# Two tiles in place of three for w2's split parts, and a sixth tile for h, in a fast-matrix-multiply feed-forward kernel

## The chip, the cores and the metric

The kernel runs on one core of a Trainium2 chip. The metric is the device time of one execution in microseconds (us); lower is better.

## The reference

The reference picks one 64x64 matrix for each of 32 samples, mixes the channels of x with it, and puts the result through a two-layer feed-forward network with a residual. All tensors are float32. Cut to what matters:

```
c   = einsum('bct,bcd->bdt', x, cond_weights[itok])   # x is 32 x 64 x 1024
h   = gelu(c @ inter_w + inter_b)                      # 1024 -> 4096
out = x + h @ output_w + output_b                      # 4096 -> 1024
```

## The kernel before

Everything but the moments at the start is matrix multiplication on TensorE (PE). Each float32 operand is split into a high part (the value rounded to the float32r type) and a low part (the value less its high part), and a product takes three matmuls: high by high, high by low, low by high. Both GEMMs are organised as fast matrix multiplications with fewer products than the plain blocking has.

**The first GEMM** makes h. Its steps are (n, c), with n from 0 to 15 (pass and group of 512 hidden columns) and c from 0 to 13. Sums and differences of blocks of h are written to two DRAM scratch tensors, `p_mem` and `q_mem`, as they are made (`keep_second` for the second pass, on the SP queue).

**The second GEMM** has 26 products t (`RANK`), each of 8 steps q (`KS`), so 208 steps. The texts number them g = 8t + q, from 0 to 207. One step multiplies a 128x512 operand of h by a 128x512 operand of w2: 4 blocks of rows (`tb`) by 3 matmuls, so 12 matmuls of 512 columns. The work of a step is spread so:

- SP (`load_h`, lines 438 to 443) loads h in pairs of steps: pair n serves steps 2n and 2n+1 and lies in one of `HRING` = 5 tiles `h_raw`. From pair 5 on, the load of pair n waits until the low parts of pair n-5 are made, since its tile is that pair's. For some products POOL adds a second block into the tile by an accumulating DMA (`add_second`, line 663).
- ACT (`high2`, lines 933 to 944) waits until step g-3 is done on PE (the ring `lhs` has `RING` = 3 tiles) and until pair g//2 is in, and writes the high part of h into `lhs` (line 939) and then that of w2 into `rhs` (line 944). `rhs` is a ring of 3 tiles as well.
- DVE (`low2`, lines 1164 to 1170) writes the low part of each (lines 1167 and 1170) when its high part is there. Behind `low2` of step g stands in DVE's order what `beside` gives it for index g-2: an update of an output tile from PSUM (`add2`, lines 1173 to 1188), or a sum of blocks of w2 for a later product (`mix`, line 1194), or nothing. For product 0 it is the trail of the first GEMM (`trail_second`, lines 1121 to 1150): up to three sums of h blocks behind a step.
- PE (`second`, lines 746 to 760) waits for both low parts of the step and runs the 12 matmuls. The PSUM banks of products t and t-2 are the same, so at the first step of product t, PE waits ahead of row block 0 for half of the updates of product t-2, and ahead of row block 2 for the rest of them. Product 16 updates four output blocks and so has 8 such instructions on DVE, indices 0 to 7 of `beside(17, i)`; the last, i = 7, stands behind `low2` of step 145, which is product 18's step 1.
- The last two steps, 206 and 207, are one piece of code, `last_two` (lines 762 to 779): the row blocks are the outer loop and the two steps the inner one, so that each output row block ends early. It waits for the low parts of both steps before its first matmul:

```
pe.wait_ge(lhs_lo, s + 2)
pe.wait_ge(rhs_lo, r + 2)
```

All waits are written out by hand. ACT and DVE work through their instructions in the order of the program, so an instruction that waits holds up all behind it on its engine. The SP queue does the same with its loads and stores; around step 0 to 12 it carries `keep_second` of group 15, the load of w2's block "30", blocks of x into the output tiles, and the pairs of h.

Of the kernel before, what the change touches and what calls it, by code (L numbers as in the profile page):

```python
# [6 lines left out]
F32R = mybir.dt.float32r  # L7
# [53 lines left out]
def build(nc, x, itok, cond_w, w1, b1, w2, b2, out):  # L61
# [12 lines left out]
    S1STEPS = GROUPS * CHUNKS  # L74
    KS = NG
    RING = 3
    WARM = 11
    HRING = 5
    PAIRS = RANK * KS // 2
    TB = 4  # L80
    NPART = 10
# [13 lines left out]
    with ExitStack() as ctx:  # L95
# [20 lines left out]
        g11, g12, g22, g21 = (at(n, 184 + 4 * i, [2, BANK]) for i, n in enumerate(("g11", "g12", "g22", "g21")))  # L116
        x1 = [at(f"x1_{j}", k, [D]) for j, k in enumerate((112, 116, 120, 124, 156, 216, 200, 184))]
        lhs = [at(f"lhs{i}", 160 + 4 * i, [2, BANK], F32R) for i in range(RING)]
        rhs = [at(f"rhs{i}", 172 + 4 * i, [2, BANK], F32R) for i in range(RING)]
        s4_w, s1_w, s2_w = (at(n, 172 + 4 * i, [KH, 2 * P]) for i, n in enumerate(("s4_w", "s1_w", "s2_w")))  # L120
        x0 = at("x0", 172, [TILES, D])
        y1_stage = [at(f"y1_stage{i}", 188 + 4 * i, [KB, P]) for i in range(2)]
        h_raw = [at(f"h_raw{i}", k, [2, BANK]) for i, k in enumerate((112, 116, 120, 124, 216))]
        part = [at(f"part{i}", 200 + 2 * i, [BANK]) for i in range(NPART)]
        part_second = {8: at("part8_second", 156, [BANK]), 9: at("part9_second", 158, [BANK])}
        y1_in = at("y1_in", 184, [4, BANK])
# [96 lines left out]
        def step2(t, q=0):  # L223
            return S1STEPS + t * KS + q
# [119 lines left out]
        def _(sp):  # L344
# [130 lines left out]
            for n in range(GROUPS):  # L475
                for c in range(CHUNKS):
                    if c == 0 and 0 < n < GROUPS - 1:
                        if n < NG - 1:
                            load_w1(n + 1)
                        elif n == NG - 1:  # L480
                            load_w1(NG + 1)
                        elif n > NG:
                            load_w1(n + 1)
                    if 0 < n <= NG:
                        keep_first(n - 1, c)
                    elif n > NG:
                        keep_second(n - 1, c)
                    if (n, c) == (1, 2):
                        for i in range(2):
                            sp.wait_ge(y1_staged[i], 32 * TB)  # L490
                        sp.dma_start(y1_in[:], y_raw_mem[0]).then_inc(y1_back, 16)
                    if y1_item(n, c) is not None:
                        keep_y1(y1_item(n, c))
                    if n == NG - 1 and c in range(4, CHUNKS, 2):
                        load_y(c // 2 - 2)
                    if n == NG and c in (0, 2):
                        load_y(5 + c // 2)
                    if n == GROUPS - 1:
                        if c == 2:
                            sp.wait_ge(lhs_lo, step1(n - 1, CHUNKS))  # L500
                            wait_kept(sp, 0, NG)
                            sp.wait_ge(c11_kept, 32 * NG)
                            wait_kept(sp, 8, NG)
                            wait_kept(sp, 9, NG)
                            for i in range(HRING):
                                load_h(i)
                        if c in (4, 6, 8):
                            sp.wait_ge(step_done, step1(n, c - 2))
                            load_w2(c // 2 - 2, ("20", "11", "10")[c // 2 - 2])
                        if c == 12:  # L510
                            sp.wait_ge(step_done, step1(n, c - 2))
                            load_x("10")

            for n in range(HRING, PAIRS):
                if n == 5:
                    for c in range(4):
                        keep_second(GROUPS - 1, c)
                    sp.wait_ge(step_done, step1(GROUPS - 1, 8))
                    load_w2(3, "30")
                if n == 6:  # L520
                    keep_second(GROUPS - 1, 4)
                    keep_second(GROUPS - 1, 5)
                if n == 7:
                    load_x("01")
                if n == 8:
                    wait_kept(sp, 8, GROUPS)
                    wait_kept(sp, 9, GROUPS)
                    for k in (1, 2, 3, 4, 5, 6, 7):
                        wait_kept(sp, k, NG)
                    for done in (c12_kept, c21_kept, c22_kept):  # L530
                        sp.wait_ge(done, 16 * NG)
                if n == 9:
                    sp.wait_ge(step_done, step1(GROUPS - 1, 12))
                    load_x("30")
                if n == 11:
                    load_x("00")
                if n == 13:
                    sp.wait_ge(rhs_lo, rhs_n(1, KS))
                    sp.wait_ge(mixed, 4)
                    load_w2(1, "31")  # L540
                if n == 16:
                    sp.wait_ge(c11_gelu, 2 * GROUPS)
                    sp.wait_ge(c12_gelu, 2 * GROUPS)
                    sp.wait_ge(c22_gelu, 2 * GROUPS)
                    load_x("31")
                if n == 18:
                    sp.wait_ge(step_done, step1(GROUPS - 1, CHUNKS))
                    load_w2(4, "01")
                if n == 20:
                    for k in range(NPART):  # L550
                        wait_kept(sp, k, GROUPS)
                    sp.wait_ge(g11_kept, 16 * NG)
                    sp.wait_ge(g22_kept, 16 * NG)
                if n == 21:
                    sp.wait_ge(lhs_lo, step1(GROUPS - 1, CHUNKS))
                    load_w2(5, "21")
                if n == 26:
                    load_x("21")
                if n == 29:
                    sp.wait_ge(rhs_lo, rhs_n(4, KS))  # L560
                    sp.wait_ge(mixed, 4 * (MIX[6] + 1))
                    load_w2(3, "00")
                if n == 34:
                    sp.wait_ge(mixed, 4 * (MIX[7] + 1))
                    load_w2(4, "20")
                if n == 37:
                    load_x("20")
                if n == 52:
                    load_x("11")
                if n == 60:  # L570
                    sp.wait_ge(acc_added, adds(12))
                    store("31")
                if n == 73:
                    sp.wait_ge(rhs_lo, rhs_n(16, KS))
                    sp.wait_ge(mixed, 4 * (MIX[18] + 1))
                    load_w2(3, "11")
                if n == 77:
                    sp.wait_ge(rhs_lo, rhs_n(17, KS))
                    load_w2(0, "10")
                if n == 80:  # L580
                    sp.wait_ge(acc_added, adds(17))
                    store("01")
                if n == 86:
                    sp.wait_ge(mixed, 4 * (MIX[20] + 1))
                    load_w2(4, "30")
                if n == 91:
                    sp.wait_ge(acc_added, adds(20))
                    store("20")
                if n == 96:
                    sp.wait_ge(acc_added, adds(21))  # L590
                    store("00")
                    store("30")
                load_h(n)
# [84 lines left out]
        def _(pe):  # L678
# [65 lines left out]
                last.then_inc(step_done, 1)  # L744

            def second(t, q):
                s, r = step2(t, q), rhs_n(t, q) % RING
                pe.wait_ge(lhs_lo, s + 1)
                pe.wait_ge(rhs_lo, rhs_n(t, q) + 1)
                for tb in range(TB):  # L750
# [11 lines left out]
            def last_two():  # L762
# [6 lines left out]
                for tb in range(TB):  # L769
                    if tb == TB - 1:  # L770
                        pe.wait_ge(acc_added, ADDED + 1)
                    for e, cols in enumerate(ENDS if tb == TB - 1 else (slice(0, BANK),)):
                        bank = bank2(t - e, tb)
                        for i in range(2):
                            for u, (a, w) in enumerate(((0, 0), (0, 1), (1, 0))):
                                last = nc.tensor.matmul(ps[:, bank, cols], lhs[(s + i) % RING][:, a, blk(tb)],  # L776
                                                        by_pairs(rhs[(r + i) % RING][:, w, :])[:, cols.start // 2:cols.stop // 2, :],
                                                        start=(e == 1 and i == 0 and u == 0),
                                                        stop=(i == 1 and u == 2), skip_group_check=True)
                        last.then_inc(tile_done, 1)  # L780
# [21 lines left out]
        def _(act):  # L802
# [128 lines left out]
                    gelu(n, 1, p, blocks(n)[2][:, p, :], c22[:, p, :], c22_gelu)  # L931

            def high2(t, q):
                s, r, n = step2(t, q), rhs_n(t, q) % RING, rhs_n(t, q) // 2
                act.wait_ge(step_done, s - RING + 1)
                act.wait_ge(h_in[n % HRING], 16 * (n // HRING + 1))
                if summed(n):
                    act.wait_ge(h_sum[n % HRING], 16 * sums(n))
                nc.scalar.activation(lhs[s % RING][:, 0, :], h_part(t, q), ACT.Copy).then_inc(lhs_hi, 1)  # L939
                if t in MIX:  # L940
                    act.wait_ge(mixed, 4 * MIX[t] + q // 2 + 1)
                elif q == 0:
# [61 lines left out]
        def _(dve):  # L1004
# [157 lines left out]
                    add_c11(n, 0)  # L1162

            def low2(t, q):
                s, r = step2(t, q), rhs_n(t, q) % RING
                dve.wait_ge(lhs_hi, s + 1)
                nc.vector.tensor_tensor(lhs[s % RING][:, 1, :], h_part(t, q), lhs[s % RING][:, 0, :].bitcast(F32),  # L1167
                                        ALU.subtract).then_inc(lhs_lo, 1)
# [194 lines left out]
```

## Time and profile before

| what | us |
|---|---|
| median of 3 runs | 1158.89 (1158.59 to 1158.95) |
| the profiled execution, its own time | 1159.22 |
| its span in the profile | 1157.4 |
| PE busy | 1152.4 |
| DVE busy | 870.2 |
| ACT busy | 561.8 |

The span is the stretch of the profile from its first to its last instruction. Busy times of the engines overlap. PE's weight loads (PEld) run beside its matmuls and are listed on their own. DMA is a mean share of 16 engines; the GB/s beside it are what they moved.

### The profile page before, as it was taken

Reading aid. Unit: us, or ns where it says so; the run is one execution under the profiler, and the core shown is the slowest. Engines: PE = TensorE matmul, PEld = TensorE weight load, DVE = VectorE, ACT = ScalarE, POOL = GpSimd, SP = SyncE. Lnnn points to the kernel's source line nnn. Section 1 sums busy time; section 2 is a strip of 40 time slices with the busy share of each in tenths; the row PEclk is TensorE's granted clock in tenths of the full one; section 3 lists DMA queues with packets and bytes.
Section 4 is the critical chain, followed back from the end, with each engine's and each line's share of the span. In section 5 each row is a group of like instructions: output and inputs, shape, how many; then the busy total and the mean of one; then the engine's idle time right before and its main releaser. Section 6 shows DMA issues by size and latency. Waiting matters only on the chain.

```text
span 1157.4 us, 15233 instructions
## 1 busy us (share of the span) xinstructions
PE 1152.4 (100%) x5468; PEld 1012.7 (87%) x5468; DVE 870.2 (75%) x1190; ACT 561.8 (49%) x963; POOL 94.7 (8%) x124
## 2 busy tenths in 40 slices
PE   9999999999999999999999999999999999999999
PEld 8988888888888888888888888888888888888887
DVE  5888787877466666666658689688899687788996
ACT  5855555555444444444445444444444444444443
POOL 3000000000001000110001121103110101101000
PEclk9999999999999999999999999999999999999999
DMA  9687768866996446764399998758963749966663
GB/s 340 202 292 247 236 265 318 280 241 237 383 399 201 133 126 145 200 198 129 96 326 303 364 315 264 222 200 181 224 187 118 193 140 253 301 196 192 200 155 118
DMA packets 118541, 263.96 MB, mean 228 GB/s; under 512 B 9890, under 2 KB 20162, under 8 KB 117058
## 3 DMA queue, kind: packets, MB, share of 16 engines
q1 hardware_dynamic: 103792, 229.14, 56.4%
q0 software_dynamic: 13824, 33.56, 17.2%
q8 instruction: 44, 0.72, 0.2%
q10 hardware_dynamic: 850, 0.28, 0.1%
q14 instruction: 31, 0.25, 0.1%
HBM read 170.67 MB, written 92.27 MB: 227 GB/s over the span
## 4 chain that ended last, share of the span: by engine, by line
PE 99%; DMA 1%; SPq 0%; DVE 0%; issue 0%
PE ps L741 50%; PE ps L757 46%; PE ps L704 1%; PE ps L689 1%; DMA x<-in_x_dram 1%; PE ps L776 0%; SPq L457 0%; SPq L458 0%; SPq L455 0%; DVE out L1331 0%
## 5 line engine op out<-in xcount | busy, mean ns | idle before, releaser
L741 PE MATMUL ps<-y,lhs 128*128 128x512 f32 x2688 | 581.6, 379 | 0.0
L741 PEld LDWEIGHTS ps<-y,lhs 128*128 128x128 f32 x2688 | 507.6, 189 | 71.8
L757 PE MATMUL ps<-rhs,lhs 128*128 128x512 f32 x2472 | 533.7, 379 | 0.0
L757 PEld LDWEIGHTS ps<-rhs,lhs 128*128 128x128 f32 x2472 | 467.2, 189 | 66.3
L939 ACT ACTIVATE lhs<-h_raw 128x512 fp32r<-128x512 f32 x208 | 131.0, 630 | 295.9 <-PE ps L757 283.0
L1167 DVE TENSOR_TENSOR lhs<-h_raw,lhs 128x512 fp32r<-128x512 f32 x208 | 143.8, 691 | 98.2 <-ACT lhs L939 98.2
L1033 DVE TENSOR_TENSOR lhs<-w_raw,lhs 128x512 fp32r<-128x512 f32 x128 | 88.5, 692 | 103.5 <-ACT lhs L840 102.0
L840 ACT ACTIVATE lhs<-w_raw 128x512 fp32r<-128x512 f32 x128 | 80.5, 630 | 163.0 <-PE ps L741 161.4
L1170 DVE TENSOR_TENSOR rhs<-w_buf,rhs 128x512 fp32r<-128x512 f32 x208 | 142.3, 684 | 0.0
L944 ACT ACTIVATE rhs<-w_buf 128x512 fp32r<-128x512 f32 x208 | 128.5, 618 | 0.0
L1033 DVE TENSOR_TENSOR lhs<-s_w,lhs 128x512 fp32r<-128x512 f32 x96 | 66.3, 691 | 68.2 <-ACT lhs L840 66.4
L840 ACT ACTIVATE lhs<-s_w 128x512 fp32r<-128x512 f32 x96 | 60.3, 629 | 113.0 <-PE ps L741 112.9
L1194 DVE TENSOR_TENSOR w_buf<-w_buf,w_buf 128x1024 f32<-128x1024 f32 x72 | 87.7, 1218 | 0.0
L1075 DVE TENSOR_TENSOR c<-ps,c 128x512 f32<-128x512 f32 x96 | 65.6, 684 | 0.0
L629 POOL DMA_DIRECT2D p_mem<-part_second x24 | 21.5, 1230 | 496.1 <-DVE part_second L1087 496.1
L845 ACT ACTIVATE c<-ps 128x512 f32<-128x512 f32 x96 | 55.6, 579 | 0.2 <-DMA p_mem<-c 0.2
L663 POOL DMA_DIRECT2D h_raw<-q_mem x32 | 28.1, 879 | 271.9 <-DMA h_raw<-p_mem 271.9
L1188 DVE TENSOR_TENSOR out<-out,ps 128x1024 f32<-128x1024 f32 x38 | 46.2, 1215 | 0.0
L1186 DVE TENSOR_TENSOR out<-ps,out 128x1024 f32<-128x1024 f32 x36 | 43.8, 1217 | 0.0
L657 POOL DMA_DIRECT2D out<-in_L_ffn_output_b_dram x32 | 28.6, 1128 | 172.6 <-DMA out<-in_x_dram 99.3
L850 ACT ACTIVATE g<-c,b_col 128x512 f32<-128x512 f32 x54 | 38.3, 709 | 0.0
L850 ACT ACTIVATE c<-c,b_col 128x512 f32<-128x512 f32 x42 | 29.8, 710 | 0.0
(56 smaller groups left out, 425.0 us busy)
## 6 DMA issues: line engine op xcount, KB each, us to landing
h_raw<-p_mem SPq DMA_DIRECT2D x80, 512.0 KB, 5.5
w_raw<-in_L_ffn_inter_w_dram SPq DMA_DIRECT2D x27, 1024.0 KB, 7.9
p_mem<-part SPq DMA_DIRECT2D x96, 256.0 KB, 6.8
w_buf<-in_L_ffn_output_w_dram SPq DMA_DIRECT2D x12, 2048.0 KB, 16.6
h_raw<-q_mem POOLq DMA_DIRECT2D x32, 512.0 KB, 7.6
y_mem<-y_out SPq DMA_DIRECT2D x28, 512.0 KB, 4.3
y<-y_mem SPq DMA_DIRECT2D x7, 2048.0 KB, 12.7
q_mem<-part SPq DMA_DIRECT2D x56, 256.0 KB, 6.9
```

The lines of the kernel that those rows point to most:

```text
L741: last = nc.tensor.matmul(ps[:, bank, :], w[:, k, :], by_pairs(y[i][:, part, k, :]), start=(i in FRESH and k == 0 and u == 0), stop=(k == ...
L757: last = nc.tensor.matmul(ps[:, bank2(t, tb), :], lhs[s % RING][:, a, blk(tb)], by_pairs(rhs[r][:, w, :]), start=(t in FRESH2 and q == 0 a ...
L840: nc.scalar.activation(split1(s, 0), w1_part(n, c), ACT.Copy).then_inc(lhs_hi, 1)
L845: nc.scalar.activation(runs(to[:, p, :]), by_runs(ps[:, bank1(n, ROLE[c // 2], p), :]), ACT.Copy).then_inc(copied, 1)
L850: nc.scalar.activation(to, of, ACT.Gelu_apprx_tanh, bias=b1_col[:, col:col + 1]).then_inc(made, 1)
L939: nc.scalar.activation(lhs[s % RING][:, 0, :], h_part(t, q), ACT.Copy).then_inc(lhs_hi, 1)
L944: nc.scalar.activation(rhs[r][:, 0, :], w2_part(t, q), ACT.Copy).then_inc(rhs_hi, 1)
L1033: nc.vector.tensor_tensor(split1(s, 1), w1_part(n, c), split1(s, 0).bitcast(F32), ALU.subtract).then_inc(lhs_lo, 1)
L1075: nc.vector.tensor_tensor(runs(tile[:, p, :]), by_runs(ps[:, bank, :]), runs(tile[:, p, :]), ALU.add).then_inc(added, 1)
L1167: nc.vector.tensor_tensor(lhs[s % RING][:, 1, :], h_part(t, q), lhs[s % RING][:, 0, :].bitcast(F32), ALU.subtract).then_inc(lhs_lo, 1)
L1170: nc.vector.tensor_tensor(rhs[r][:, 1, :], w2_part(t, q), rhs[r][:, 0, :].bitcast(F32), ALU.subtract).then_inc(rhs_lo, 1)
L1194: nc.vector.tensor_tensor(w2_buf[to][:, pair], w2_buf[a][:, pair], w2_buf[b][:, pair], op).then_inc(mixed, 1)
```

## The change

The ring `rhs` has two tiles in place of three (`RHS_RING` = 2), and ACT waits, ahead of the high part of w2 for step g, until step g-2 is done on PE; it stands after the high part of h of the same step. The 4 KiB that were `rhs`'s third tile become the sixth of `h_raw` (`HRING` = 6). On the SP queue the first five pairs of h are issued where they were; pair 5 is issued where it was, now after a wait for the first GEMM's step (15, 5), and without the wait for pair 0; from pair 6 on, the load of pair n waits for the low parts of pair n-6.

```
-    HRING = 5
+    RHS_RING = 2
+    HRING = 6
...
-        rhs = [at(f"rhs{i}", 172 + 4 * i, [2, BANK], F32R) for i in range(RING)]
+        rhs = [at(f"rhs{i}", 172 + 4 * i, [2, BANK], F32R) for i in range(RHS_RING)]
...
-        h_raw = [at(f"h_raw{i}", k, [2, BANK]) for i, k in enumerate((112, 116, 120, 124, 216))]
+        h_raw = [at(f"h_raw{i}", k, [2, BANK]) for i, k in enumerate((112, 116, 120, 124, 216, 180))]
...
-                            for i in range(HRING):
+                            for i in range(HRING - 1):
                                 load_h(i)
...
-            for n in range(HRING, PAIRS):
+            for n in range(HRING - 1, PAIRS):
                 if n == 5:
+                    sp.wait_ge(lhs_lo, step1(GROUPS - 1, 6))
                     for c in range(4):
                         keep_second(GROUPS - 1, c)
...
             def high2(t, q):
-                s, r, n = step2(t, q), rhs_n(t, q) % RING, rhs_n(t, q) // 2
+                s, r, n = step2(t, q), rhs_n(t, q) % RHS_RING, rhs_n(t, q) // 2
                 act.wait_ge(step_done, s - RING + 1)
...
                 nc.scalar.activation(lhs[s % RING][:, 0, :], h_part(t, q), ACT.Copy).then_inc(lhs_hi, 1)
+                if rhs_n(t, q) >= RHS_RING:
+                    act.wait_ge(step_done, s - RHS_RING + 1)
```

In `second`, `last_two` and `low2` the index into `rhs` is taken modulo `RHS_RING` as well.

## Rows read from the trace of the kernel before

**Rows 1.** The page: span, granted clock and DMA by slice.

```profile
span 1157.4 us, 15233 instructions
...
PEclk9999999999999999999999999999999999999999
DMA  9687768866996446764399998758963749966663
```

**Rows 2.** The chain that ended last, in order of time: start, us, what.

```profile
615.80 533.54 PE ps L757 x2472
1149.34 5.24 PE ps L776 x30
```

**Rows 3.** The costliest groups: two lines of the second GEMM (busy, mean ns | idle before).

```profile
L939 ACT ACTIVATE lhs<-h_raw 128x512 fp32r<-128x512 f32 x208 | 131.0, 630 | 295.9 <-PE ps L757 283.0
L1170 DVE TENSOR_TENSOR rhs<-w_buf,rhs 128x512 fp32r<-128x512 f32 x208 | 142.3, 684 | 0.0
```

**Rows 4.** Timeline around step 207's operands: start, us, engine, line.

```profile
1146.79 0.63 ACT L939 ACTIVATE lhs<-h_raw 128x512 fp32r<-128x512 f32 x1 [1.44 <-PE ps L757]
1147.33 0.62 ACT L944 ACTIVATE rhs<-w_buf 128x512 fp32r<-128x512 f32 x1
1147.45 0.69 DVE L1167 TENSOR_TENSOR lhs<-h_raw,lhs 128x512 fp32r<-128x512 f32 x1 [1.30 <-ACT lhs L939]
1148.06 0.68 DVE L1170 TENSOR_TENSOR rhs<-w_buf,rhs 128x512 fp32r<-128x512 f32 x1
1148.97 1.05 PEld L776 LDWEIGHTS ps<-rhs,lhs 128*128 128x128 f32 x5
1149.18 1.03 PE L776 MATMUL ps<-rhs,lhs 128*128 128x512 f32 x4
```

**Rows 5.** PE alone, at the start of the span: a start after a wait.

```profile
10.37 10.98 PE L689 MATMUL ps<-wdiag,x 128*128 128x128 f32 x96 [0.28 <-DMA x<-in_x_dram]
```

**Rows 6.** PEld alone, the same stretch.

```profile
10.36 10.79 PEld L689 LDWEIGHTS ps<-wdiag,x 128*128 128x128 f32 x96 [0.47 <-DMA x<-in_x_dram]
```

**Rows 7.** Timeline around step 145's operands and the update behind them.

```profile
986.21 0.63 ACT L939 ACTIVATE lhs<-h_raw 128x512 fp32r<-128x512 f32 x1 [1.44 <-PE ps L757]
...
987.48 0.68 DVE L1170 TENSOR_TENSOR rhs<-w_buf,rhs 128x512 fp32r<-128x512 f32 x1
...
988.08 1.22 DVE L1188 TENSOR_TENSOR out<-out,ps 128x1024 f32<-128x1024 f32 x1
988.80 0.63 ACT L939 ACTIVATE lhs<-h_raw 128x512 fp32r<-128x512 f32 x1 [1.44 <-PE ps L757]
```

**Rows 8.** Timeline of DVE in product 0, steps 3 to 5.

```profile
620.30 1.28 DVE L1087 TENSOR_TENSOR part<-g,g 128x512 f32<-128x512 f32 x2
621.62 0.69 DVE L1083 TENSOR_TENSOR part<-part,g 128x512 f32<-128x512 f32 x1
622.23 0.69 DVE L1167 TENSOR_TENSOR lhs<-h_raw,lhs 128x512 fp32r<-128x512 f32 x1
622.83 0.69 DVE L1170 TENSOR_TENSOR rhs<-w_buf,rhs 128x512 fp32r<-128x512 f32 x1
623.44 0.68 DVE L1087 TENSOR_TENSOR part<-part,g 128x512 f32<-128x512 f32 x1
...
625.84 0.68 DVE L1170 TENSOR_TENSOR rhs<-w_buf,rhs 128x512 fp32r<-128x512 f32 x1
```

**Rows 9.** Timeline of the SP queue, the issues of the same stretch.

```profile
618.43 0.32 SPq L365 DMA_DIRECT2D q_mem<-part  x1
618.79 0.46 SPq L447 DMA_DIRECT2D w_buf<-in_L_ffn_output_w_dram  x1
619.30 3.92 SPq L443 DMA_DIRECT2D h_raw<-p_mem  x1
```

**Rows 10.** Timeline of ACT and DVE when pairs 5 and 6 come in.

```profile
638.32 0.63 ACT L939 ACTIVATE lhs<-h_raw 128x512 fp32r<-128x512 f32 x1 [3.19 <-DMA h_raw<-p_mem]
...
644.27 0.63 ACT L939 ACTIVATE lhs<-h_raw 128x512 fp32r<-128x512 f32 x1 [3.76 <-DMA h_raw<-p_mem]
...
645.54 0.68 DVE L1170 TENSOR_TENSOR rhs<-w_buf,rhs 128x512 fp32r<-128x512 f32 x1
```

**Rows 11.** Busy time by stretch around pair 5's way in (engines, PEclk, DMA share, GB/s).

```profile
615.00:620.00 5.00, 5.00 (x25) 4.38 (x24) 3.42 (x7) 3.47 (x7) 1.79 (x2) 1.00 1.09 352
620.00:625.00 5.00, 5.00 (x25) 4.38 (x24) 4.96 (x9) 2.31 (x4) 0.00 (x0) 1.00 1.22 183
```

More of the change, by code:

```diff
@@ L746, in second @@
             def second(t, q):
-                s, r = step2(t, q), rhs_n(t, q) % RING
+                s, r = step2(t, q), rhs_n(t, q) % RHS_RING
                 pe.wait_ge(lhs_lo, s + 1)
@@ L776, in last_two @@
                                 last = nc.tensor.matmul(ps[:, bank, cols], lhs[(s + i) % RING][:, a, blk(tb)],
-                                                        by_pairs(rhs[(r + i) % RING][:, w, :])[:, cols.start // 2:cols.stop // 2, :],
+                                                        by_pairs(rhs[(r + i) % RHS_RING][:, w, :])[:, cols.start // 2:cols.stop // 2, :],
                                                         start=(e == 1 and i == 0 and u == 0),
@@ L1164, in low2 @@
             def low2(t, q):
-                s, r = step2(t, q), rhs_n(t, q) % RING
+                s, r = step2(t, q), rhs_n(t, q) % RHS_RING
                 dve.wait_ge(lhs_hi, s + 1)
```

## The prediction

> **What bounds the kernel now.** I read the chain that ended last first. From 615.80 us on it is nothing but PE: 2472 matmuls of the second GEMM in 533.54 us, then the 30 of `last_two` in 5.24 us [rows 2]. That is 0.2158 us for each matmul and 2.590 us for each step of 12, with no wait between any two of them. The granted clock is full in every slice, which is the 2.4 GHz level [rows 1]. So PE bounds the second GEMM alone. The reader is to see there that nothing in this stage can be won by feeding PE sooner: h is never late for PE, though it is for ACT. The only thing that the change can do to the stage is to leave PE without work.
>
> Then I looked at how much earlier than needed each operand is there, since the change takes that away. The first matmul of step 206 starts at 1149.18 [rows 4], so that step g starts at P(g) = 1149.18 - 2.590 x (206 - g). Step 207's operands show the pattern: ACT starts the high part of h at 1146.79, which is P(205) + 0.20, the end of step 204's last matmul. In the steady state ACT has been waiting for just that (283.0 us in all [rows 3]). The high part of w2 follows 0.54 later, DVE's first low part 0.66 after ACT's start, its second at 1148.06, done at 1148.74. PE would want it for step 207 only at P(207), and the weight load ahead of it 0.21 earlier (1148.97 against 1149.18), at 1151.56. An ordinary step therefore has 2.8 us in hand.
>
> **What the change removes: one step of lead for w2.** ACT may now write w2's high part for step g only at the end of step g-2, P(g-1) + 0.20. DVE's low part can start 0.66 later, at P(g-1) + 0.86, and ends at P(g-1) + 1.54 (0.68 of work [rows 4]). The weight load of step g is due at P(g-1) + 2.38. So an ordinary step still has 0.84 us in hand. DVE's order holds too: low part of w2 (0.61 from start to start), an update or mix (1.22 [rows 7]), low part of h for the next step (0.61) make 2.43 us against 2.59, the same three instructions as before, only turned round. ACT has 1.1 us of work per step. All of that is covered, and costs nothing. Three places are not ordinary.
>
> **Place one, the end.** `last_two` wants the w2 parts of steps 206 and 207 both before its first matmul. Before, both were there at 1148.74, ahead of 1148.97 [rows 4]. Now ACT may begin w2's high part for step 207 only when step 205 is done, at 1149.18 + 0.20 = 1149.38. DVE starts 0.66 later at 1150.04, ends at 1150.72, and PE sees it 0.03 later, as DVE sees ACT's end (0.66 less 0.63). Nothing covers it: steps 206 and 207 are the only work that PE has left, and both are behind the wait. The first matmul starts at 1150.75 if it follows the weight load at once, or at 1150.96 if it needs the 0.21 of the steady rows. Cost 1.57 to 1.78 us. After a wait the rows show a matmul 0.01 behind its weight load (10.37 against 10.36 [rows 5, 6]), so I take a value nearer the lower end, 1.62. The updates behind it on DVE, and the stores, move with it.
>
> **Place two, product 18.** The last update of product 16 stands on DVE behind `low2` of step 145. In step 144 PE wants that update ahead of row block 2. P(144) is 988.60; the seventh matmul is due 6 x 0.2158 later at 989.90, its weight load at 989.69. Before, the update ran from 988.08 to 989.30 [rows 7], with 0.39 us in hand. Now the low part of w2 for step 145 waits for the end of step 143, which ACT's row shows at 988.80 [rows 7]. DVE starts it at 989.46, the update 0.60 later (987.48 to 988.08 [rows 7]) at 990.06, and ends at 991.28. PE goes on at 991.31 to 991.52 and not at 989.90: 1.41 to 1.62 us, taken as 1.46. What is queued behind the waiting ACT instruction is the high part of h for step 146 (due much later) and behind it on DVE the update itself, which is what hurts. I went through the other products: with one, two or three targets the last update stands behind step 3, 5 or 7 of the product before, so there is a whole step or more left. This is the one place. The mixes for the next product's w2 are made two steps before ACT wants them and keep over 2 us in hand.
>
> **Place three, product 0.** There DVE has three extra sums behind step 3 and three behind step 4, so five instructions a step, 0.60 to 0.61 each from start to start, about 3.0 us against PE's 2.59 [rows 8]. The lead of 2.8 took that up. Now w2's low part of step 3 starts at 623.41 - 2.59 + 0.86 = 621.68 in place of 619.70. The three sums follow (the third 1.32 after the first, as from 620.30 to 621.62 [rows 8]) at 622.28 to 623.60, then step 4's low parts at 624.21 and 624.81, ended at 625.50; due is P(4) - 0.21 = 625.79. Three more sums, then step 5's at 627.22 and 627.82, ended at 628.50 against 628.38 due. PE's matmul starts 0 to 0.15 late; I take 0.1. After it DVE has one sum behind step 5 and catches up.
>
> **What it adds: a sixth tile for h.** It lets the loads of pairs from 6 on go out up to one pair (5.18 us) sooner. PE waits for none of them now, so the gain is 0. The bound above is 0 too, the bound below is what the SP queue may lose. Pair 5 was not held by its tile: its issue stands at 619.30 directly behind w2's block "30" (618.79), and that behind a sum of h kept at 618.43 [rows 9]. In the changed kernel that sum is made about 2 us later, since it stands behind w2's low part of step 2, and all three issues move to about 620.4 to 621.3. Pair 5 landed at 638.3, pair 6 at 644.27, both later than ACT wanted them [rows 10]. Pair 6 is the critical one: its step's w2 low part is done at 645.54 + 0.68 = 646.22, and PE's weight load for step 12 is due at 646.51. There are 0.3 us in hand, in both kernels alike, as late h drags w2's high part behind it. So a load that lands 2 us later would cost PE 1.7. I take 0, for two reasons: the DMA engines are loaded fully in that stretch (share 1.09 and 1.22 [rows 11]) and hold a backlog that a later issue doesn't change, and pair 5's issue already took 3.92 us [rows 9], so the queue was pushing back. Both ends, 0 and 1.7, are kept for the range. Other w2 loads that wait for `rhs_lo` or `mixed` move by about 2 us and are due tens of us later.
>
> **Sum.** 1.62 + 1.46 + 0.1 = 3.2 us (2.98 to 3.55 by the bounds). PE is the chain throughout, so each idle stretch adds in full. The profiled execution should go from a span of 1157.4 to 1160.6, its own time from 1159.22 to 1162.4; the profiled execution is 0.33 above the median, and against the median of 1158.89 the forecast is 1162.1.
>
> [...] The rows of steps 144 and 206 say that two tiles are one too few at these two places. [...]
>
> **The rivals.**
>
> *Only the end costs (6%).* If DVE had the update of step 145 out of the way some other way, as with the low part of w2 for step 145 not being held, the middle wait would go. It needs 1.4 us that I find nowhere, since the wait, the copy and two DVE instructions follow strictly. It gives 1158.9 + 1.7 = 1160.6, within what can be told from no change, so this ends on the other side.
>
> *Two tiles suffice everywhere (3%).* It would need more than 1.7 us of further lead in `last_two`, so a wait for the low parts that PE meets late; the rows show it meeting that wait ahead of 1148.97. 1158.9.
>
> *h comes later in product 1 (15%).* The issues of w2's block "30" and pair 5 slip by 2 us and the queue is not full enough to take that up. For it speaks that the throughput in the stretch falls to 183 GB/s [rows 11], so what keeps the engines loaded there is other traffic. It decides from a slip of 0.3 us on and adds 0.3 to 1.7: 1162.4 to 1163.8. A later pair behind a w2 load could do the same.
>
> *The clock falls (3%).* If the granted clock dropped to 1.2 GHz after the wait in step 206, the last 5.24 us [rows 2] would take twice as long: 1167.3. Nothing in the rows speaks for it: the clock was full in all slices [rows 1], the first one with its short waits included. The waits of the new kernel are longer than those.
>
> *A gain (1%).* It would have to come from a wait of PE that the chain shows; it shows none in this stage.
>
> **How the numbers follow.** My forecast has 72%: 1162.1, its own range 1161.7 to 1162.6. The range that should hold 8 in 10 reaches down part of the way to the case of the end alone and up over late h: 1161.0 to 1163.9. A measurement of this kernel can tell some 0.2%, 2.3 us, from no change. Slower by more than that (over 1161.2) are the forecast, late h and the clock, 90%; within it are the two cases with a hidden wait, 9%; faster 1%.
>
> **What would show it.** In the profile of the changed kernel: PE (L757) idle once around step 144 for about 1.45 us, released by DVE's L1188; PE (L776) idle for about 1.6, released by DVE's L1170; PE's busy time unchanged. ACT's wait for PE moves for the most part from the high part of h to that of w2, and DVE's low part of w2 gets waits for ACT where it had none [rows 3]. In product 0 a PE gap of at most 0.15 before step 5. If PE has a gap around step 12 or another that ends in an h load, the late h is real. The prediction is wrong if PE has no gap at step 144, or if gaps show at every step.

## The result and the profile after

The changed kernel takes 1162.5 us (median of 8 runs, 1162.16 to 1162.77) against 1158.92 for the kernel before (8 runs, 1158.47 to 1159.54). The ratio is 1.0031, with a 95% interval of 1.0021 to 1.0040: it is slower by 3.6 us. The forecast was 1162.1. In two of the runs below, those with pairs 5 and 6 sooner and with one sum moved, one execution of 11 took 3005 and 3822 us for a reason that isn't known; the medians given are of all 11.

The span of the profiled execution is 1161.0, 3.6 more than before. First the page of the changed kernel, with the groups that answer to [rows 3]:

```profile
span 1161.0 us, 15385 instructions
...
PEclk9999999999999999999999999999999999999999
...
L948 ACT ACTIVATE rhs<-w_buf 128x512 fp32r<-128x512 f32 x208 | 131.0, 630 | 292.3 <-PE ps L759 292.3
L1174 DVE TENSOR_TENSOR rhs<-w_buf,rhs 128x512 fp32r<-128x512 f32 x208 | 143.9, 692 | 96.8 <-ACT rhs L948 96.5
L1171 DVE TENSOR_TENSOR lhs<-h_raw,lhs 128x512 fp32r<-128x512 f32 x208 | 142.2, 684 | 5.0 <-ACT lhs L941 5.0
L941 ACT ACTIVATE lhs<-h_raw 128x512 fp32r<-128x512 f32 x208 | 128.6, 618 | 7.2 <-DMA h_raw<-p_mem 5.3
```

The waits have changed sides. ACT waits for PE ahead of w2's high part, 292.3 us in all where it used to wait 283.0 ahead of h's. DVE's low part of w2 waits for ACT 96.5 us where it had no wait at all, and the low part of h, which used to wait 98.2, waits 5.0. None of that is time by itself. What counts is PE's own row, from its timeline, which before was one unbroken piece up to the last 30 matmuls [rows 2]:

```profile
615.35 374.94 PE L759 MATMUL ps<-rhs,lhs 128*128 128x512 f32 x1734
991.57 159.55 PE L759 MATMUL ps<-rhs,lhs 128*128 128x512 f32 x738 [1.28 <-DVE out L1192]
1152.66 5.46 PE L778 MATMUL ps<-rhs,lhs 128*128 128x512 f32 x30 [1.54 <-DVE rhs L1174]
```

Those rows show no shorter gap. The rows of the weight loads end where there is a longer idle time, and show two more places:

```profile
628.34 18.00 PEld L759 LDWEIGHTS ps<-rhs,lhs 128*128 128x128 f32 x84 [0.28 <-issue]
646.85 343.04 PEld L759 LDWEIGHTS ps<-rhs,lhs 128*128 128x128 f32 x1590 [0.51 <-issue]
991.57 159.15 PEld L759 LDWEIGHTS ps<-rhs,lhs 128*128 128x128 f32 x738 [1.68 <-DVE out L1192]
1152.63 5.30 PEld L778 LDWEIGHTS ps<-rhs,lhs 128*128 128x128 f32 x30 [1.91 <-issue]
```

There are four: at step 5, at step 12, in the middle of step 144, and ahead of step 206. How much time each took is best read from ACT: w2's high part waits for the end of a PE step, and in the steady rows starts 0.20 after the start of the next one. These are ACT's and DVE's rows at the two long ones, from the timeline, in two pieces:

```profile
989.03 0.63 ACT L948 ACTIVATE rhs<-w_buf 128x512 fp32r<-128x512 f32 x1 [1.44 <-PE ps L759]
...
989.70 0.69 DVE L1174 TENSOR_TENSOR rhs<-w_buf,rhs 128x512 fp32r<-128x512 f32 x1 [0.16 <-ACT rhs L948]
990.30 1.21 DVE L1192 TENSOR_TENSOR out<-out,ps 128x1024 f32<-128x1024 f32 x1
...
993.17 0.63 ACT L948 ACTIVATE rhs<-w_buf 128x512 fp32r<-128x512 f32 x1 [2.98 <-PE ps L759]
...
1151.16 0.63 ACT L948 ACTIVATE rhs<-w_buf 128x512 fp32r<-128x512 f32 x1 [1.44 <-PE ps L759]
1151.82 0.69 DVE L1174 TENSOR_TENSOR rhs<-w_buf,rhs 128x512 fp32r<-128x512 f32 x1 [1.30 <-ACT rhs L948]
```

Step 144 lasted 993.17 - 989.03 = 4.14 us in place of 2.59: 1.55 lost. Step 206 was due at 1151.16 - 0.20 = 1150.96 and started at 1152.66: 1.70 lost. Read in the same way, step 5 lost 0.15 (ACT's starts are 628.50 and 631.24, 2.74 apart) and step 12 0.37 (646.78 and 649.74, 2.96 apart). From step 206's start to the start of the last update it is 5.50 us (to 1158.16) where it was 5.42, 0.08 more. The second GEMM itself began at 615.35, 0.29 sooner than at 615.64. That comes from the first 11 us of the execution, where PE waited three times for x in the kernel before ([rows 5] is the last of them) and not in this one; over all profiles here the second GEMM begins between 615.15 and 616.02. The account closes: -0.29 + 0.15 + 0.37 + 1.55 + 1.70 + 0.08 = 3.56 of 3.6.

PE's busy time was forecast unchanged and is 1154.0 against 1152.4. Of the 1.6 us more, 1.0 lies in the first 60 us, where those waits for x are missing. The other 0.6 is lost time of the second GEMM that counts as busy: the matmul before a gap lasts longer in the rows, so that they show 1.28 and 1.54 us of idle time where the first matmul behind the gap was 1.45 and 1.70 late, and the gaps at steps 5 and 12 don't show as idle time of the matmuls.

### The profile page after: what moved, and what is told of

It reads as the page before. It is cut to its first block, busy times and chain, and to the rows that moved or that the text cites. A ratio compares the mean times of both kernels' runs of the same rounds, so it can differ in the third digit from the quotient of the medians.

```text
span 1161.0 us, 15385 instructions
## 1 busy us (share of the span) xinstructions
PE 1154.0 (99%) x5468; PEld 1013.4 (87%) x5468; DVE 870.5 (75%) x1190; ACT 562.0 (48%) x963; POOL 94.5 (8%) x124
## 4 chain that ended last, share of the span: by engine, by line
PE 97%; DMA 1%; DVE 1%; issue 0%; ACT 0%; DVEq 0%; ACTq 0%
PE ps L743 50%; PE ps L759 44%; DMA h_raw<-p_mem 1%; PE ps L691 1%; PE ps L706 1%; PE ps L778 0%; PE ps L786 0%; DVE part L1091 0%; DVE rhs L1174 0%; ACT rhs L948 0%; DVE lhs L1171 0%; DVE out L1192 0%; DVE part L1087 0%; ACT lhs L941 0%; DVE out L1335 0%
## 5 line engine op out<-in xcount | busy, mean ns | idle before, releaser
L948 ACT ACTIVATE rhs<-w_buf 128x512 fp32r<-128x512 f32 x208 | 131.0, 630 | 292.3 <-PE ps L759 292.3
L1174 DVE TENSOR_TENSOR rhs<-w_buf,rhs 128x512 fp32r<-128x512 f32 x208 | 143.9, 692 | 96.8 <-ACT rhs L948 96.5
L941 ACT ACTIVATE lhs<-h_raw 128x512 fp32r<-128x512 f32 x208 | 128.6, 618 | 7.2 <-DMA h_raw<-p_mem 5.3
```

The source lines that it names most:

```text
L948: nc.scalar.activation(rhs[r][:, 0, :], w2_part(t, q), ACT.Copy).then_inc(rhs_hi, 1)
L1174: nc.vector.tensor_tensor(rhs[r][:, 1, :], w2_part(t, q), rhs[r][:, 0, :].bitcast(F32), ALU.subtract).then_inc(rhs_lo, 1)
```

## The experiments

Medians stand beside those of the kernel before from the same sessions (1158.95 to 1159.03 us). One profiled execution of each shows the gaps; it can differ from the median of its runs.

**The wait alone, in the kernel before.** Three tiles for w2, five for h, all loads as before:

```
                 nc.scalar.activation(lhs[s % RING][:, 0, :], h_part(t, q), ACT.Copy).then_inc(lhs_hi, 1)
+                if rhs_n(t, q) >= 2:
+                    act.wait_ge(step_done, s - 1)
```

> The kernel before (three tiles for w2's parts, five for h) with one line more: ACT waits for step g-2 ahead of w2's high part of every step g. Theory (the lost step of lead is the whole cost, the tile of h gains nothing): PE waits at the same places as in the changed kernel, about 1.5 us in step 144, 1.7 ahead of step 206, 0.1 to 0.2 at step 5, and perhaps 0.4 at step 12; time 1158.9 + 3.2 to 3.8 = 1162.1 to 1162.7, the same as the changed kernel within 0.3. Rival (where the tiles lie, or the order of loads that the sixth tile brings, makes part of the cost): the time is over 0.8 us away from the changed kernel's 1162.5. Second rival (the sixth tile gives something back): this kernel is slower than 1163.3.

Measured: 1162.44 us, ratio 1.0029 (1.0017 to 1.0040), the changed kernel's time. PE and PEld of its timeline:

```profile
991.87 159.80 PE L757 MATMUL ps<-rhs,lhs 128*128 128x512 f32 x738 [1.28 <-DVE out L1190]
1153.21 5.46 PE L776 MATMUL ps<-rhs,lhs 128*128 128x512 f32 x30 [1.54 <-DVE rhs L1172]
...
629.02 361.17 PEld L757 LDWEIGHTS ps<-rhs,lhs 128*128 128x128 f32 x1674 [0.28 <-issue]
...
1016.73 134.55 PEld L757 LDWEIGHTS ps<-rhs,lhs 128*128 128x128 f32 x624 [0.39 <-issue]
```

The same 1.28 and 1.54, and the same 0.28 at step 5. So the wait is the cost; of where the tiles lie in memory, and of the order of loads that the sixth tile brings, these runs show no cost. The small one at step 12 is not there, and another stands at 1016.73, in product 19. ACT's row shows that it comes from a late second block of h:

```profile
1014.65 0.63 ACT L939 ACTIVATE lhs<-h_raw 128x512 fp32r<-128x512 f32 x1 [2.42 <-DMA h_raw<-q_mem]
```

**The wait at two steps alone.**

```
+                if (t, q) in ((18, 1), (25, 7)):
+                    act.wait_ge(step_done, s - 1)
```

> The kernel before with the wait for step g-2 ahead of w2's high part in steps 145 and 207 alone. Theory (two places make the cost and add up): a gap of PE of 1.4 to 1.6 us in step 144 and of 1.6 to 1.75 ahead of step 206, none elsewhere; 1158.9 + 3.1 = 1162.0. Rival (the loss is spread over the steps, many small waits too short to be seen): under 1160.9.

Measured: 1162.36 us, ratio 1.0028 (1.0017 to 1.0039); span 1160.6. PE's timeline has the two gaps, of the same lengths to 0.01, and none else:

```profile
991.26 159.55 PE L757 MATMUL ps<-rhs,lhs 128*128 128x512 f32 x738 [1.28 <-DVE out L1190]
1152.35 5.46 PE L776 MATMUL ps<-rhs,lhs 128*128 128x512 f32 x30 [1.54 <-DVE rhs L1172]
```

Of all the steps that lose a step of lead, these two make 3.3 of the 3.6 us. The many small waits of the rival are not there.

**The end repaired, in the changed kernel.** The four row blocks of the last two steps are taken in another order, so that 9 matmuls of step 206 stand ahead of the wait for step 207:

```
-                pe.wait_ge(lhs_lo, s + 2)
-                pe.wait_ge(rhs_lo, r + 2)
-                for tb in range(TB):
+                pe.wait_ge(lhs_lo, s + 1)
+                pe.wait_ge(rhs_lo, r + 1)
+                for i in range(2):
+                    if i == 1:
+                        pe.wait_ge(lhs_lo, s + 2)
+                        pe.wait_ge(rhs_lo, r + 2)
+                    for tb in range(TB - 1):
...
+                for tb in range(TB - 1, TB):
```

> The changed kernel with the last two steps' matmuls in another order: PE waits for step 206's operands alone, runs step 206 for the first three row blocks (9 matmuls, 1.94 us), waits for step 207's, runs it for the same blocks, and ends with the fourth as before. Theory: 9 matmuls cover the 1.70 us gap; no gap before step 206 and none after the ninth matmul; time 1162.5 - 1.7 = 1160.8. The tail may lose up to 0.1, as the first blocks end later. Rival (the time lost at the end is not this wait, or comes back as a longer tail): 1162.2 or more.

Measured: 1160.68 us, ratio 1.0015 (1.0006 to 1.0024), 1.8 us less than the changed kernel; expected was 1.7. The timeline shows the weight loads without a pause and DVE's w2 part made meanwhile:

```profile
1150.61 3.86 PEld L777 LDWEIGHTS ps<-rhs,lhs 128*128 128x128 f32 x18
...
1151.68 0.69 DVE L1185 TENSOR_TENSOR rhs<-w_buf,rhs 128x512 fp32r<-128x512 f32 x1 [1.30 <-ACT rhs L959]
...
1154.71 1.50 PE L789 MATMUL ps<-rhs,lhs 128*128 128x256 f32 x12
```

The tail is no longer: from the first of the 30 matmuls to the last update's start it is 1156.24 - 1150.82 = 5.42, as in the kernel before.

**Product 16's updates one step sooner, in the changed kernel.**

```
+                    if (t == 17 and q >= 1) or (t, q) == (18, 0):
+                        beside(17, rhs_n(t, q) - rhs_n(17, 1))
-                    if t > 0 or q >= 2:
+                    elif (t, q) != (18, 1) and (t > 0 or q >= 2):
                         beside(*divmod(rhs_n(t, q) - 2, KS))
```

> The changed kernel with product 16's eight updates one step sooner on DVE: behind the low parts of steps 137 to 144 in place of 138 to 145, so that the last no longer stands behind w2's low part of step 145. Theory: the update ends at about P(144) + 0.1, due is P(144) + 1.1: no gap in step 144, time 1162.5 - 1.55 = 1161.0, and the gaps at steps 5, 12 and 206 stay. Rival (PE would then wait for step 145's operands themselves, as DVE is full there): the gap moves to step 145 and the time stays within 0.5 of 1162.5.

Measured: 1161.00 us, ratio 1.0017 (1.0008 to 1.0026), just the 1161.0 expected. PE's timeline is one piece up to step 206:

```profile
615.50 533.85 PE L759 MATMUL ps<-rhs,lhs 128*128 128x512 f32 x2472
1150.89 5.46 PE L778 MATMUL ps<-rhs,lhs 128*128 128x512 f32 x30 [1.54 <-DVE rhs L1174]
```

The gap did not move to step 145. DVE does the same work, with the eight updates one step sooner. The gap at step 5 is in the weight loads of this profile (0.29); the one at step 12, which the expectation also kept, is not.

**Both repairs.**

> The changed kernel with both repairs, the order of the last two steps and product 16's updates a step sooner. Theory (the two waits are the loss and are independent): no gap in step 144 nor before step 206; what stays is the 0.15 us at step 5 and, in an execution where pair 6 lands late, up to 0.4 at step 12; 1162.5 - 1.7 - 1.55 = 1159.2. Rival (something else of the change costs, hidden so far behind the two waits): 1160 or more.

Measured: 1159.12 us, ratio 1.0001 (0.9992 to 1.0010). The two gains add up, and nothing else of size was hidden behind them. Its weight loads still show the two small gaps:

```profile
628.42 18.00 PEld L759 LDWEIGHTS ps<-rhs,lhs 128*128 128x128 f32 x84 [0.29 <-issue]
646.86 502.32 PEld L759 LDWEIGHTS ps<-rhs,lhs 128*128 128x128 f32 x2328 [0.45 <-issue]
```

**Both repairs, five tiles for h.** The same, with `HRING = 5` and the loads as before.

> As the run with both repairs, but with five tiles for h and its loads issued as in the kernel before, so the change's first half alone. Theory (the sixth tile gains nothing where PE doesn't wait for h): within 0.4 us of the run with six tiles, about 1159.2 to 1159.6; a late h may show as a gap of PE of up to 0.4 in one place. Rival (with the shorter lead for w2 the sixth tile is needed): PE waits for h in several places and the time is over 1160.

Measured: 1159.42 us, ratio 1.0004 (0.9995 to 1.0013). Beside 1159.12 with six tiles the intervals overlap; a gain of the sixth tile of the size of that difference, 0.3 us, can be neither shown nor excluded. Its profile has the gap at step 5 and no other.

**Both repairs, pairs 5 and 6 of h sooner.**

```
+                        if c == 6:
+                            sp.wait_ge(lhs_lo, step1(n, 6))
+                            load_h(5)
                         if c in (4, 6, 8):
...
                     for c in range(4):
+                        if c == 3:
+                            load_h(6)
                         keep_second(GROUPS - 1, c)
...
-                load_h(n)
+                if n not in (5, 6):
+                    load_h(n)
```

> Both repairs, and the sixth tile put to use: pair 5 is issued at step (15, 6), ahead of w2's block 11, and pair 6 ahead of w2's block 30 and of the sum that stands before it. Theory: ACT no longer waits for pairs 5 and 6, no gap at step 12 in any execution; the 0.15 at step 5 stays; 1159.0 to 1159.2, as there is nothing more to win from h. Rival (the two earlier pairs push w2's blocks or x back, and ACT or DVE waits for one of those): PE shows a gap in product 0 or 1, over 1159.8.

Measured: 1159.16 us, ratio 1.0001 (0.9992 to 1.0011). In its profile ACT waits for no load of h at all. The weight loads show the gap at step 12 gone and that at step 5 still there:

```profile
615.01 12.92 PEld L764 LDWEIGHTS ps<-rhs,lhs 128*128 128x128 f32 x60
628.22 520.45 PEld L764 LDWEIGHTS ps<-rhs,lhs 128*128 128x128 f32 x2412 [0.29 <-issue]
```

**The same, one sum moved from behind step 4 to behind step 5.**

```
-                    combine(4, n, part[4][:], h32, ALU.add)
+                    if n < GROUPS - 1:
+                        combine(4, n, part[4][:], h32, ALU.add)
                 if c == 5:
+                    if n == GROUPS - 1:
+                        combine(4, n, part[4][:], h32, ALU.add)
```

> The same with one of the three sums behind step 4 of product 0 moved behind step 5. Theory (DVE's five instructions a step in steps 3 and 4 make the gap at step 5): w2's low part of step 5 ends 0.60 sooner, no gap at step 5, so no gap of PE in the whole second GEMM; 1158.9, the time of the kernel before and not less. Rival (the gap at step 5 comes from the start of the GEMM, not from DVE): it stays at 0.15.

Measured: 1159.05 us, ratio 1.0000 (0.9991 to 1.0010). The chain that ended last has PE's 2472 matmuls in one piece of exactly the length of [rows 2]:

```profile
615.64 533.54 PE ps L764 x2472
1149.18 3.88 PE ps L782 x18
1153.06 1.35 PE ps L794 x12
```

PE then has no gap left to close in this stage. No version beat the kernel before; this one ties it.

**Four tiles for h, in the kernel before.** `HRING = 4`, three tiles for w2.

> The kernel before (three tiles for w2's parts) with four tiles for h in place of five; pair 4 is loaded from the later part of the SP queue. It asks how much the number of tiles for h matters at all. Theory (the fifth tile already has room to spare except where the DMA engines are full): a load goes out up to 5.18 us later than before; from about 700 us on it still lands in time and PE shows no gap; in products 0 to 2 ACT waits for more pairs, and PE loses 0 to 2 us, so 1158.9 to 1161. Rival (tiles for h matter throughout, so that the sixth should have gained something too): gaps in many products, over 1164.

Measured: 1164.54 us, ratio 1.0047 (1.0033 to 1.0060), runs from 1163.0 to 1165.3. That misses the theory's 0 to 2 us, and passes the rival's 1164, but not in the rival's way: PE has gaps in three places only, two short ones in product 1, 0.53 us together, and one long one in product 19. Between them 142 steps ran without any. PE and PEld of the timeline:

```profile
646.76 368.02 PE L757 MATMUL ps<-rhs,lhs 128*128 128x512 f32 x1704 [0.30 <-DVE rhs L1170]
1017.08 136.60 PE L757 MATMUL ps<-rhs,lhs 128*128 128x512 f32 x624 [2.31 <-DVE rhs L1170]
...
1017.05 136.23 PEld L757 LDWEIGHTS ps<-rhs,lhs 128*128 128x128 f32 x624 [2.68 <-DVE lhs L1167]
```

ACT's row shows what came late: the second block of pair 77, which POOL adds by a DMA after the load has landed.

```profile
1014.98 0.63 ACT L939 ACTIVATE lhs<-h_raw 128x512 fp32r<-128x512 f32 x1 [6.79 <-DMA h_raw<-q_mem]
```

The chain that ended last goes back from there through both DMAs:

```profile
993.76 12.65 DMA h_raw<-p_mem
...
1006.76 8.11 DMA h_raw<-q_mem
```

It is the load that was slow, 12.65 us from issue to landing where the median of its kind is 5.2. SP had issued a 2 MB block of w2 at 988.07, ahead of it, and the DMA share from 1010 on was still over 1; that this block is what slowed the load is not shown.

It is the place where with five tiles the small gap of the first experiment stood. The gap cost 2.54 us (1017.08 - 646.76, less 142 x 2.590), but the 52 steps behind it took 1.76 more than 134.68 us. The stretches of the same execution show why (engines, PEclk, DMA share, GB/s):

```profile
1010.00:1014.00 4.00, 4.00 (x21) 3.49 (x20) 0.00 (x0) 0.00 (x0) 0.28 (x1) 1.00 1.06 272
1014.00:1017.00 3.00, 0.77 (x4) 0.34 (x2) 1.36 (x3) 2.02 (x4) 0.00 (x0) 1.00 1.08 225
1017.00:1020.00 3.00, 2.92 (x7) 2.41 (x8) 3.00 (x4) 1.32 (x3) 0.00 (x0) 0.52 0.71 143
1020.00:1021.00 1.00, 1.00 (x4) 0.78 (x4) 1.00 (x3) 0.00 (x0) 0.00 (x0) 0.73 0.81 299
1021.00:1024.00 3.00, 3.00 (x15) 2.65 (x14) 3.00 (x6) 1.15 (x2) 0.00 (x0) 1.00 0.13 52
```

After the gap the granted clock was half, the 1.2 GHz level, until about 1020.5: 7 matmuls in the 3 us from 1017 where 14 are usual. The account of this execution is 0.53 + 2.54 + 1.76, less 0.49 by which its second GEMM began sooner: 4.3 us, as the spans say (1161.7 and 1157.4). At 1163.56 us it is 1.0 below the median of its runs; where the others lost that is not known.

## Why the prediction was right

**PE bounds the stage, and each of its gaps adds in full.** Right. The account of the gaps closes to 0.04 us on the span, and each repair gave back what its gap had taken.

**Ordinary steps keep 0.84 us in hand and cost nothing.** Right: the wait at two steps alone costs what the wait at all of them costs, within the runs. The Trainium skill (Trainium Kernel Development and Optimization, section Best Practices) advises double-buffering, to overlap DMA with compute; it doesn't say when two buffers are enough, and this ring is filled by engines and not by a DMA. Here two tiles were enough for an ordinary step and one too few at the two places, which lost 1.55 and 1.70 us.

**The end, 1.57 to 1.78, taken as 1.62.** The mechanism was right, the value 0.16 too low. Measured are 1.70 to the first matmul and 0.08 in the tail behind it. ACT's start, 0.20 after the step's start, and DVE's, 0.66 later, were as forecast. What I had too short is the last hop: DVE ends at 1152.51 and the first matmul starts at 1152.66, 0.15 later; the 1.62 allowed 0.08 (1150.72 to 1150.80). The rest of the miss is the 0.08 in the tail. That tail may be the first weight load, which no longer runs under a matmul; no run tests it.

**Product 18, 1.41 to 1.62, taken as 1.46.** Right in place and kind; measured 1.55. PE went on 0.06 after DVE's update had ended (991.51, 991.57), and the step as a whole lost 0.1 more than the 1.45 by which its seventh matmul was late (due at 990.12). I had chosen the value near the lower end in both cases by a row of 128x128 matmuls behind a DMA [rows 5, 6], which was the wrong neighbour: the middle of the range would have been nearer.

**Product 0, 0 to 0.15, taken as 0.1.** Measured 0.15, at step 5 as forecast, and gone when DVE had one sum less behind step 4.

**The sixth tile gains nothing.** Right in the time: 1162.44 without it, 1162.5 with it. The profiles show that it is not idle, though. In the six profiles of kernels with six tiles, POOL's adding DMA for pair 77 starts between 1000.11 and 1000.97, and ACT has no wait there. In the four with five tiles it starts at 1001.13 (the kernel before), 1002.39, 1003.50 and 1005.57, and in three of them ACT waits for it, 2.16 to 2.42 us. PE lost by it once, in the run with the wait alone (0.39 between weight loads); the run with both repairs and five tiles had the wait and no gap. So the sixth tile takes a risk away that is too small to be seen in the medians.

**Late h in product 1, taken as 0 and kept as a rival with 15%.** This was partly so, and it is the one term that was put at nothing and was not nothing. The measured 1162.5 lies in the forecast's own range and in this rival's as well, so the time alone does not tell them apart; the profile shows both. Pair 6 came in at 644.77 and not 644.27, while the step that wants it was 0.14 sooner, so the 0.3 us in hand were used up and step 12 lost 0.37. That gap is in two of the four profiles of kernels with six tiles and the order of loads of the change (the changed kernel and the one with both repairs); in the other two, with one repair each, pair 6 landed in time. The w2 block and pair 5 were issued 1.7 us later (620.49 and 620.97 against [rows 9]), about as forecast; most of that was taken up, for pair 5 landed at 638.41 against 638.32 [rows 10]. Pair 6's own issue was not late: it stands at 628.57, 0.28 sooner than the 628.85 of before, and of the four profiles the one with the latest issue (628.97) has it in first (643.64). The w2 block and pair 5 were issued later in those as well where pair 6 landed in time. What made its transfer take longer in two of them is not shown. With pairs 5 and 6 issued sooner the gap was gone.

**The clock.** It stayed at 1.00 in both long gaps of the changed kernel, as forecast. That the rival was a real one shows in the run with four tiles.

The forecast missed by 0.4 us in all: 0.16 and 0.09 at the two long waits, 0.05 at step 5, 0.37 at step 12, less 0.29 by which the second GEMM began sooner in that execution. Each term was too low, so that it came as near as this owes something to those 0.29, which are luck.

## What to carry to other kernels

When a buffer is taken from a ring, don't ask whether the ordinary step has room for it. List the places where the consumer wants an operand, or something queued behind it on the producer, earlier than the ordinary step does: a wait for two steps at once, a half-step deadline, an overfull step. Here each cost its own lateness, and each was repaired by order alone. And before a tile is given to a ring, look for the wait of the bounding engine that it would remove; here there was none.

## What the runs showed of the hardware

The granted clock stayed at 1.00 through idle times of 1.28 and 1.54 us between matmuls (1.68 and 1.91 between weight loads) in five profiles, four times each. Behind one of 2.31 (2.68), in the one profile that has such a gap, it was 0.52 over the next 3 us. That cost 1.76 us in the steps behind the gap, beside the gap's own 2.54.

A DMA issue on the SP queue can be held. Pair 5's took 3.92 us before, and 2.08 in the changed kernel, where it was issued 1.7 us later; both ended within 0.2 us of each other (623.22 and 623.05), where the issue ahead of it on the queue, w2's block "30", had taken 0.46 and 0.44.
